# A GRU scan after attention: logistic gates on ScalarE, and the input side as full-width matmuls

## What is computed

```python
B, T, D = 4, 512, 512
x = x + attention(x, cond)          # 16 heads, modulated rms norm, then o + o @ W_out
def cell(h, x_t):                    # then a GRU over the 512 positions, h starts as cond
    gi = x_t @ W_ih + b_ih
    gh = h @ W_hh + b_hh
    i_r, i_z, i_n = split(gi, 3); h_r, h_z, h_n = split(gh, 3)
    r = sigmoid(i_r + h_r)
    z = sigmoid(i_z + h_z)
    n = tanh(i_n + r * h_n)
    return (1 - z) * n + z * h
x = x + scan(cell, cond, x)          # every state is added to its position
```

## Time and profile before

| | |
|---|---|
| median of 3 runs | 2332.82 us (2330.83 to 2335.31) |
| the profiled execution | 2332.44 us, of which the span from first to last instruction is 2330.3 us |
| granted clock of TensorE, mean | 0.994 |
| busy: PE matmul, weight load, VectorE, ScalarE, GpSimd | 95%, 73%, 61%, 53%, 9% of the span |
| attention and setup | 0 to about 648 us |
| the 512 steps | from about 649 us to the end |

### The profile page before, as it was taken

The page is one execution under the profiler, slowest core; times in us unless marked ns, Lnnn a source line. Parts: engine busy times, 40 slices in busy tenths (PEclk is TensorE's granted clock), DMA queues, the critical chain, the costliest instruction groups (busy, mean ns, idle before and its releaser), DMA issues.

```text
span 2330.3 us, 131116 instructions
## 1 busy us (share of the span) xinstructions
PE 2215.0 (95%) x58384; PEld 1695.6 (73%) x58384; DVE 1418.2 (61%) x5488; ACT 1243.2 (53%) x5114; POOL 202.6 (9%) x223
## 2 busy tenths in 40 slices
PE   5999999999799999999999999999999999999988
PEld 3656656566478887878788887878788787878776
DVE  2665746656356666666666666666666666666665
ACT  2655746556145555555555555555555555555554
POOL 4314233142200000000000000000000000000000
PEclk9999999999899999999999999999999999999999
DMA  6000000000110000000000000000000000000000
GB/s 208 1 1 19 2 19 1 1 1 2 67 33 21 18 26 17 27 20 21 28 16 26 18 26 17 27 19 21 29 16 25 18 26 18 26 20 21 25 5 13
DMA packets 41093, 55.08 MB, mean 24 GB/s; under 512 B 9424, under 2 KB 34000, under 8 KB 40528
## 3 DMA queue, kind: packets, MB, share of 16 engines
q1 hardware_dynamic: 34112, 38.81, 5.4%
q0 software_dynamic: 1584, 7.73, 0.9%
q10 hardware_dynamic: 4832, 0.15, 0.1%
HBM read 29.90 MB, written 16.78 MB: 20 GB/s over the span
## 4 chain that ended last, share of the span: by engine, by line
PE 80%; DVE 7%; ACT 6%; issue 2%; POOL 2%; DMA 1%; POOLq 1%; ACTq 1%; SPq 0%; DVEq 0%
PE ps L458 53%; PE ps L305 8%; PE ps L444 7%; PE ps L356 5%; PE ps L379 4%; DVE rT L801 3%; PE ps L393 2%; PE ps L431 2%; DVE xb L796 2%; ACT r_pair L619 2%; ACT r_pair L616 2%; ACT xb L627 2%; DVE v_pair L786 2%; POOL qk_rs L285 1%; POOLq L62 1%
## 5 line engine op out<-in xcount | busy, mean ns | idle before, releaser
L458 PE MATMUL ps<-wqkv,xb 128*4 128x128 f32 x49152 | 1488.9, 273 | 53.9 <-DVE xb L796 41.2
L458 PEld LDWEIGHTS ps<-wqkv,xb 128*4 128x4 f32 x49152 | 1215.7, 87 | 339.1 <-DVE xb L796 313.8
L801 DVE STREAM_TRANSPOSE rT<-ps 128x128 f32<-128x128 f32 x512 | 162.0, 316 | 341.5 <-PE ps L458 341.5
L616 ACT ACTIVATE r_pair<-rT 128x16 f32<-128x16 f32 x512 | 112.3, 219 | 456.2 <-DVE rT L801 456.2
L781 DVE STREAM_TRANSPOSE znT<-ps 128x128 f32<-128x128 f32 x1024 | 312.2, 305 | 63.2 <-PE ps L458 1.1
L625 ACT ACTIVATE t_z<-znT 128x8 f32<-128x8 f32 x1024 | 214.6, 210 | 252.0 <-DVE znT L781 252.0
L796 DVE TENSOR_TENSOR_SCAN xb<-z_trip,xb 128x24 f32<-128x24 f32 x1024 | 212.9, 208 | 122.7 <-ACT xb L627 6.1
L627 ACT ACTIVATE xb<-v_pair 128x16 f32<-128x16 f32 x1024 | 222.8, 218 | 52.8 <-DVE v_pair L786 2.2
L786 DVE TENSOR_TENSOR_SCAN v_pair<-r_pair,znT 128x16 f32<-128x16 f32 x1024 | 195.9, 191 | 71.8 <-ACT r_pair L619 2.3
L444 PE MATMUL ps<-wih,x1T 128*32 128x256 f32 (+1 forms) x4096 | 231.3, 326 | 0.0
L584 ACT ACTIVATE probs<-ps,negmax 128x512 f32<-128x512 f32 x256 | 172.6, 685 | 68.6 <-DVE negmax L704 68.6
(11 more groups left out here) (77 smaller groups left out, 1106.3 us busy)
## 6 DMA issues: line engine op xcount, KB each, us to landing
gi_spill<-gi_image SPq DMA_DIRECT2D x64, 192.0 KB, 2.0
seeds<-gi_spill SPq DMA_DIRECT2D x228, 32.0 KB
seeds<-gi_spill SPq DMA_DIRECT2D x284, 16.0 KB
xb<-in_x SPq DMA_DIRECT2D x4, 1024.0 KB, 5.7
out<-xb SPq DMA_DIRECT2D x64, 64.0 KB, 2.2
wqkv<-in_L_cond_W_qkv SPq DMA_DIRECT2D x1, 3072.0 KB, 11.9
wih<-in_L_cond_W_ih POOLq DMA_DIRECT2D x1, 3072.0 KB, 16.2
wqkv<-in_L_cond_W_hh POOLq DMA_DIRECT2D x1, 3072.0 KB, 10.7
```

Source lines behind the costliest of these rows:

```text
L458: last = nc.tensor.matmul(ps[QD * j:QD * j + B, bank, 0:P], hist_flat[:, first:first + 3 * B - 2:3], weights, start=False, stop=False, ski ...
L801: nc.vector.transpose(rT[:], ps[:, r_bank, 0:P]).then_inc(s["rT_ready"], 1)
```

## The change

Two things are changed. The gates: ScalarE computes the logistic function directly. For r this replaces two ScalarE instructions by one; for z it replaces ScalarE's tanh and VectorE's multiply and add by one ScalarE instruction that writes `z_trip`. The order of the two waits ahead of `candidate(0)` is exchanged. The input side: GpSimd copies the 128 rows of a block (4 sequences by 32 positions) into a new tile `x1_rows`; they are the weights of one matmul of 192 columns on the whole array, without a tile position, and every one of the 32 steps has one of them (`LEAD` goes from 12 to 20, so 20 of block 1's are made ahead). Its result has the 128 rows on the partitions and one of four column groups in each evacuation, so the biases have to lie on all 128 partitions (12 loads in place of 8, and an addition on GpSimd in batch row 1).

```diff
-LEAD = 12
+LEAD = 20
-        b_in = sb("b_in", [P, GCOL])
+        b_in = sb("b_in", [P, 4, GCOL])
+        x1_rows = sb("x1_rows", [P, 2, KT, P])
@@ GpSimd, the bias loads and the row copies
-                for tile, source in ((b_in, b_ih), (b_hid, b_hh)):
-                    pool.dma_start(tile[quarter, :].rearrange("p (n x) -> p n x", x=QD),
-                                   source.rearrange("(n j x) -> j n x", j=4, x=QD)[j].partition_broadcast(QD)
-                                   ).then_inc(ld_bias, 16)
+                pool.dma_start(b_hid[quarter, :].rearrange("p (n x) -> p n x", x=QD),
+                               by_column(b_hh).partition_broadcast(QD)).then_inc(ld_bias, 16)
+                for tile, source in ((b_in, b_ih), (b_hh_rows, b_hh)):
+                    pool.dma_start(tile[:, j, :].rearrange("p (n x) -> p n x", x=QD),
+                                   by_column(source).partition_broadcast(P)).then_inc(ld_bias, 16)
+            def first_rows(batch):
+                await_on_pool(s["x1_ready"], (batch + 2) * KT)
+                for n in range(2):
+                    nc.gpsimd.tensor_copy(x1_rows[:, n, :, BLK * batch:BLK * batch + BLK],
+                                          x1T[:, :, batch, BLK * n:BLK * n + BLK]).then_inc(s["block_rows"], 1)
@@ in the loop over 16 projection tiles n of batch row b
+                    if n == 2 and b > 0:
+                        first_rows(b - 1)
+                    if n == 4 and b == 1:
+                        await_on_pool(ld_bias, 16 * 12)
+                        nc.gpsimd.tensor_tensor(b_in[:, :, 0:2 * P], b_in[:, :, 0:2 * P], b_hh_rows[:, :, 0:2 * P],
+                                                ALU.add).then_inc(s["bias_ready"], 1)
@@ GpSimd after the load of W_hh
+            first_rows(B - 1)
+            for n in range(2, N_BLK):
+                await_on_pool(s["gi_done"], 4 * (n - 1))
+                nc.gpsimd.tensor_copy(x1_rows[:, n % 2].rearrange("p k (b t) -> p (k b) t", b=B),
+                                      x1T[:, :, :, BLK * n:BLK * n + BLK].rearrange("p k b t -> p (k b) t")
+                                      ).then_inc(s["block_rows"], 1)
@@ TensorE
+            def gi_piece(n, q):
+                j, half, k = q // 8, q // 4 % 2, q % 4
+                chunks = slice(2 * half, 2 * half + 2)
+                weights = wih[:, k, :].rearrange("p (g c j x) -> p g c j x", c=KT, j=4, x=QD)[:, :, chunks, j, :]
+                image = ps[:, gi_bank(n, j), 0:GCOL].rearrange("p (g c) -> p g c", g=3)[:, :, 2 * QD * half:2 * QD * half + 2 * QD]
+                return nc.tensor.matmul(image, x1_rows[:, n % 2, k, :], weights, start=(k == 0), stop=(k == KT - 1),
+                                        skip_group_check=True)
@@ TensorE, at the end of each step
-                if n < N_BLK and q < 6 * B and step + LEAD >= 12:
-                    b, i = divmod(q, 6)
...
-                    for k, gates in PIECES[i]:
-                        last = gi_piece(k, gates, b, n, GI_BANKS[b % 2])
+                if n < N_BLK:
+                    if q == 0:
+                        pe.wait_ge(s["block_rows"], rows_copied(n))
+                    if q % 8 == 0:
+                        pe.wait_ge(s["gi_evac"], 4 * n + q // 8)
+                    last = gi_piece(n, q)
@@ ScalarE
-                                     ACT.Tanh, scale=0.5).then_inc(s["tr_done"], 1)
-                act.wait_ge(s["tr_done"], step + 1)
-                nc.scalar.activation(r_pair[:, :, 1], r_pair[:, :, 1], ACT.Copy, bias=0.5,
-                                     scale=0.5).then_inc(s["r_ready_gru"], 1)
+                                     ACT.Sigmoid).then_inc(s["r_ready_gru"], 1)
-                    nc.scalar.activation(t_z[:, half, :], znT[:, half, 0:16:2], ACT.Tanh, scale=0.5).then_inc(s[tz_name], 1)
+                    nc.scalar.activation(z_trip[:, 8 * half:8 * half + 8, 2], znT[:, half, 0:16:2],
+                                         ACT.Sigmoid).then_inc(s[z_name], 1)
@@ VectorE, half A (half B loses its z_gate in the same way)
+                dve.wait_ge(s["znaT_ready"], step + 1)
                 dve.wait_ge(s["r_ready_gru"], step + 1)
-                dve.wait_ge(s["znaT_ready"], step + 1)
                 candidate(0).then_inc(s["va_done"], 1)
-                dve.wait_ge(s["tza_done"], step + 1)
-                z_gate(0).then_inc(s["za_done"], 1)
```

More of the change, by code:

```diff
@@ L144, in attention_gru_kernel @@
         X_BANKS = (PO, PJ[0], PJ[1], PM)
-        GI_BANKS, ROW_BANK = (6, 7), 7
+        GI_BANK, ROW_BANK = 6, 7
+        PREFILLED = LEAD
         (ld_cond, ld_emb, ld_wqkv, ld_wout, ld_wih, ld_whh, ld_bias, ld_gi0, ld_gi1, ld_gi2, ld_gi3, ld_x, ld_g, st_gi, st_out) = (
@@ L198, in _, with spill @@
                     sp.dma_start(xb[:], x[b + 1].rearrange("(t p) f -> p t f", p=P)).then_inc(ld_x, 16)
[L201 to L203 removed]
+            def spill(n, j):
+                sp.wait_ge(s["gi_evac"], 4 * n + j + 1)
+                if n >= 2 and j == 0:
                     for wave in range(4):
                         sp.wait_ge(ld_gi[wave], gi_landed(n - 2, wave))
[L206 removed]
+                sp.dma_start(gi_spill[n % 2, j], gi_image[:, j, :]).then_inc(st_gi, 16)
             def fetch(n, wave, j):
+                rows = gi_spill[n % 2, j].rearrange("(b t) c -> b t c", b=B)
                 for first, done, count in seed_parts(n, wave):
[L210 removed]
+                    steps = slice(done, done + count)
                     sp.dma_start(seeds[QD * j:QD * j + B, first:first + count, 0:2 * P],
[L212 removed]
+                                 rows[:, steps, 0:2 * P]).then_inc(ld_gi[wave], 16)
                     sp.dma_start(seeds[QD * j + B:QD * j + 2 * B, first:first + count, 2 * P:3 * P],
[L214 removed]
+                                 rows[:, steps, 2 * P:3 * P]).then_inc(ld_gi[wave], 16)
             def send_rows(m, b):
@@ L220, in _ @@
             sp.wait_ge(s["seeds_clear"], 2)
-            for b in range(B):
-                spill(0, b)
-            sp.wait_ge(st_gi, 16 * B)
+            for j in range(4):
+                spill(0, j)
+            sp.wait_ge(st_gi, 16 * 4)
             for wave in range(4):
@@ L226, in _ @@
                     fetch(0, wave, j)
-            spill(1, 0)
+            for j in range(PREFILLED // 8):
+                spill(1, j)
             for step in range(T):
@@ L233, in _ @@
                     if due == 0:
-                        sp.wait_ge(st_gi, 16 * B * (n + 1))
+                        sp.wait_ge(st_gi, 16 * 4 * (n + 1))
                     sp.wait_ge(s["seeded"], step + 2)
                     fetch(n, wave, j)
-                ahead, due = divmod(step + LEAD - 7, BLK)
-                if ahead + 1 < N_BLK and due % 6 == 0 and due < 6 * B and step + LEAD - 7 >= 6:
-                    spill(ahead + 1, due // 6)
+                ahead, due = divmod(step + LEAD - 8, BLK)
+                if ahead + 1 < N_BLK and due % 8 == 0:
+                    spill(ahead + 1, due // 8)
                 if m > 0 and 24 <= u < 24 + B:
@@ L437, in _, with gi_bank, rows_copied @@
             pe.wait_ge(ld_whh, 16)
[L441 to L451, removed]
+            def gi_bank(n, j):
+                return GI_BANK + j % 2 if n == 0 or n == 1 and 8 * j + 8 <= PREFILLED else GI_BANK
+            def rows_copied(n):
+                return 2 * B + max(n - 1, 0)
+            def gi_piece(n, q):
[5 more added lines that the diff above has]
+                                        skip_group_check=True)
             def hidden_side(bank, gates, chunks, step, half):
@@ L471, in _ @@
             last.then_inc(s["banks_open"], 1)
[L472 to L476, removed]
-                        last = gi_piece(k, gates, b, n, GI_BANKS[b % 2])
-                last.then_inc(s["gi_done"], 1)
+            pe.wait_ge(s["block_rows"], 2 * B)
+            for n, count in ((0, BLK), (1, PREFILLED)):
+                for q in range(count):
+                    if q % 8 == 0 and 4 * n + q // 8 >= 2:
+                        pe.wait_ge(s["gi_evac"], 4 * n + q // 8 - 1)
+                    last = gi_piece(n, q)
+                    if q % 8 == 7:
+                        last.then_inc(s["gi_done"], 1)
             def rows_of_block(m, c):
@@ L501, in _ @@
                 n = ahead + 1
-                if n < N_BLK and q < 6 * B and step + LEAD >= 12:
-                    b, i = divmod(q, 6)
[L504 to L507, removed]
-                    for k, gates in PIECES[i]:
-                        last = gi_piece(k, gates, b, n, GI_BANKS[b % 2])
-                    if i == 5:
+                if n < N_BLK:
[3 more added lines that the diff above has]
+                        pe.wait_ge(s["gi_evac"], 4 * n + q // 8)
+                    last = gi_piece(n, q)
+                    if q % 8 == 7:
                         last.then_inc(s["gi_done"], 1)
@@ L750, in _, with evacuate_gi @@
             dve.sem_inc(s["h_b"], 1)
```

(17 more changed lines are left out.)

34 lines of the change are left out of this document (14 added, 20 removed).

## The result

The changed kernel takes 2339.3 us (median of 12 runs, 2337.8 to 2340.4), the kernel before 2333.8 us on the same chips (12 runs); the ratio is 1.0024, 95% interval 1.0015 to 1.0033. I had forecast 2312 us and a gain of 0.9%. The profiled execution took 2338.6 us, its span from first to last instruction 2336.7 us, 6.4 more than before, at a granted clock of 0.993 (before 0.994).

What follows compares the result with a forecast made beforehand. The 512 steps bound the kernel, through the gates' loop of 3.25 us, TensorE's own being 3.05. Forecast: 2332.4 - 52 + 11 + 5 + 1.3 + 10 + 4 = 2312 us, range 2278 to 2355.

Steps and rivals of the forecast that it cites:

- rivals C: GpSimd: bias loads cost 21 us and row copies 14 us, giving 2332 us in all; chance 0.11.
- Rival D: Candidate A gains nothing, for example a wait costing VectorE another 0.06 us: gates' loop 3.20 us, 2336 us; chance 0.09.
- The gates, 3.25 to 3.14: Gates' loop of each step falls from 3.25 to 3.14 us; of r's 0.25 us only 0.07 comes through.
- TensorE's loop, 3.15: TensorE's loop with an input piece: 3.15 us, a change into the whole array at 0.11; gain 46 us over 460 steps.
- The change out, 0.09 from the nearest row: TensorE going from the whole array back to column groups after the input matmul: 0.09 us extra.
- Rival B: Each array-mode change on TensorE waits for the last pass: loop 3.47 us, 2459 us (2386 with one); chance 0.15.
- `rows_of_block`: Its four matmuls on TensorE, hidden before, now bare: 0.22 us in each of 52 steps, +11 us.
- GpSimd's bias loads, +10: Before attention's first scores: loads with 1536 runs take 2.5 us each in proportion, making GpSimd 10 us late.
- GpSimd's other work ahead of tile 4, +4: In attention: row copies in three batch rows (1.7 us) and an addition in row 1 (2.3 us), +4 us.
- Copies, +5: GpSimd's 13 row copies within the steps delay VectorE by 0.4 us each, +5 us; bounds 0 and 14.
- Table load, +1.3: ScalarE needs one more function-table load before the first step, +1.3 us once, 0 if in a wait.
- Rival E: Logistic function and tanh in different ScalarE tables: four changes a step, five us a step, near 4900 us; chance 0.03.

Runs made afterwards that it cites:

- gates_only: The kernel before with only the change's gates and order of waits, input side left in column groups: 2281.4 us, ratio 0.9779 to the kernel before.
- direct_old_waits: groups_direct with the two waits ahead of candidate A in the old order, r first and then the transposition: 2311.8 us, ratio 0.9897 to the kernel before.
- groups: The changed kernel with each whole-array input matmul made as four 192-column matmuls in column groups: 2284.0 us, ratio 0.9785 to the kernel before.
- groups_direct: groups with the four matmuls' weights taken straight from x1T, without GpSimd's row copies: 2282.0 us, ratio 0.9774 to the kernel before.
- input_only: The changed kernel with the old gates, the gates' part of the change undone: 2353.2 us, ratio 1.0082 to the kernel before.
- narrow_weights: The changed kernel with 32 of the 128 rows as weights, leaving out sequences 1 to 3's input side (not the full GRU): 2276.8 us, one run.

## Why the prediction was wrong

The measured 2339 us lie inside my range of 2278 to 2355, by luck: I had reached up there for rivals C and D, and neither is what happened. The kernel got slower where I forecast a gain, and one term did it.

- *The gates, 3.25 to 3.14:* right, step by step (3.143 in gates_only, 3.142 in the last steps of the changed kernel). Of the 0.25 us that r gives up only 0.07 comes through, as worked out, and the order of the waits is what lets it (direct_old_waits). Rival D was near this: its 0.06 for a wait is real, but in the old order.
- *TensorE's loop, 3.15:* the step that failed is the price of a change in, 0.11. It is 0.11 + 0.105: the first pass waits for its own 128 columns of weights. By my own line the case was decided from 0.10 us more than my price. I read 0.20 from start to start and took the spacing behind it for the usual one. It could be read beside the row used: two passes of 384 columns took 0.91; that source line's passes last 0.49 at the least and median, so the starts are 0.42 apart, where 24 of them in 7.91 us are (7.91 - 0.49) / 23 = 0.32 apart. The wait is inside the first pass's record and not ahead of its start (0.43 for the first and 0.33 for the second in the changed kernel), which is why 0.20 from start to start doesn't show it. Of the kernel before, by source line and in the timeline:
```profile
L356 PE MATMUL ps<-wqkv,xnT x512: 486/486/1009, 32.3 to 560.9; 128*128 128x384 f32 x171
...
32.29 7.91 PE L356 MATMUL ps<-wqkv,xnT 128*128 128x384 f32 x24
```
- *The change out, 0.09 from the nearest row:* right (0.26 = 0.163 + 0.093). Rival B, a whole wait for the last pass, wasn't it: in 0.20, out 0.26. Nor does it hide in the first pass's record: with 64 columns of weights 0.20 + 0.05 = 0.25 is still under the 0.27 that the last pass lasts, though ends of passes are modelled. The rule of the Trainium skill (TensorEngine Tiling, Key Properties) is that a change of mode drains TensorE. This trace agrees that a change costs time, 0.11 and 0.09, and shows less than a drain to the recorded end of the last pass. What the array does in these 0.11 and 0.09 us no run shows; they are the same for 64 and 128 columns of weights. With the first pass's 0.105 it is 2.62 + 0.33 + 0.31 = 3.26.
- *`rows_of_block`:* 52 x 0.24 = 12.7 us for a forecast of 11; the premise, that they were hidden before, is right (3.254 with and without them).
- *GpSimd's bias loads, +10:* wrong, 0. 1536 runs take 1.03 to 1.06 us, not 2.5, and GpSimd was idle again before VectorE released it; in proportion to the runs was the wrong reading. GpSimd in the changed kernel:
```profile
33.66 1.06 POOL L281 DMA_DIRECT2D b_hh_rows<-in_L_cond_b_hh  x1
35.28 0.24 POOL L302 TENSOR_SCALAR qk_ms<-qk_ss 128x8 f32<-128x8 f32 x1 [0.55 <-DVE qk_ss L720]
```
- *GpSimd's other work ahead of tile 4, +4:* right in size. From the first scores of batch row 0 to those of row 1 it is 150.2 us in place of 145.9, over the whole of attention and setup 3.4 (first r at 654.17, before 650.72).
- *Copies, +5:* about 1.2 us, on the mechanism below. *Table load, +1.3:* it comes at 652.99 and ends at 654.27, before the transposition of the first r has ended (654.49), so it falls in a wait: 0. By the Trainium skill (ScalarE: Activation LUTs, section on table sets) a set holds the logistic function and tanh together. The trace agrees: the changed kernel has this load and the one of attention at 16.75, and none in the 512 steps, where the two functions alternate. Rival E is out.
- *The sum of the steps:* 408 ordinary ones 3.258 in place of 3.254, +2; `rows_of_block` + 13; copies + 1; 51 last ones - 6; and the other longer steps, 8 us before, about 1 now, - 7. Together + 3, and 3.1 measured (2328.28 - 654.17 against the earlier trace rows); with attention's 3.4 this is the 6.4 of the span.

Two errors of opposite sign stood in the sum: - 50 us of gain that wasn't there (460 x 0.108), and about 15 of losses on GpSimd and in the table that weren't there either; the 7 us fewer in longer steps were not forecast at all. (The prediction's "12 us of piece steps" is a slip; its 10.3 us are right, and nothing rests on the 12.)

Three versions beat both kernels: gates_only, groups and groups_direct, 2.2 to 2.3% faster than before. Between them the runs don't decide. The gates' gain is in all three; that the input side made in every step adds anything to it, no run shows.

## What to carry to other kernels

When two loops are near each other (here 3.05 and 3.25 us), price a change against the second one to the last tenth of a microsecond, and count on nothing being shared between steps of a recurrence. A float32 matmul over the whole array between matmuls in column groups cost 0.31 us beyond its columns here, at 128 columns of weights; as four matmuls in column groups it cost only the columns. Read the spacing behind the first pass too, not only the one ahead of it.

## What the runs showed of the hardware

GpSimd's copy of 512 elements holds up VectorE's scan of two SBUF tensors. In the changed kernel it is that of the new state in 12 of the 13 steps with a copy, and in one that of the candidate (0.64 in place of 0.19); in input_only it is the z gate in all 13. The changed kernel, then input_only, each at such a copy:
```profile
901.83 0.61 POOL L323 COPY x_rows<-x1T 128x512 f32<-128x512 f32 x1 [104.83 <-PE ps L477]
902.08 0.42 DVE L816 TENSOR_TENSOR_SCAN xb<-z_trip,xb 128x24 f32<-128x24 f32 x1 [0.28 <-ACT xb L651]
```
```profile
901.83 0.61 POOL L324 COPY x_rows<-x1T 128x512 f32<-128x512 f32 x1 [104.99 <-PE ps L478]
901.92 0.55 DVE L819 TENSOR_SCALAR z_trip<-t_z 128x8 f32<-128x8 f32 x1
902.58 0.21 DVE L823 TENSOR_TENSOR_SCAN xb<-z_trip,xb 128x24 f32<-128x24 f32 x1
```
The scan takes 0.42 in place of 0.21 and ends 0.06 after the copy (902.44). In input_only the z gate stands still, 0.55 in place of 0.17, and the step is 3.63 us in place of 3.26; in the changed kernel 3.35. So the same copy costs 0.37 or 0.09, by which VectorE instruction it meets and how much room is behind it. In groups, where the gates set the step, it is 0.04.

What stays open: the longer steps outside `rows_of_block`, mostly 0.1 to 0.4 us each, 24 before and 53 in gates_only. In one of the kernel before (r at 906.67) candidate A started 0.39 us behind the last of its inputs, where 0.04 is usual. No run looked for their cause. The changed kernel has 22, of which 13 are those of the copies. The other nine (steps 19, 44, 154, 215, 264, 276, 325, 447 and 472) are long in groups, groups_direct and narrow_weights too, so they go with the place in the program and not with chance. A bound on TensorE that hides such steps isn't needed to explain their small number either: narrow_weights, where the gates set the step, has only 16.
